# A routed mixture of experts on one core: one table value per tile, expert weights in two unpadded parts, rows as 16-bit halves

## What is computed

```python
h = _layernorm(x, axis=-1) * (1 + cb) + sb
x = x + gb * _L0_ffn_ref(h, ...)

# _L0_ffn_ref: 32 experts in 4 groups, M = 176 hidden values
scores = sigmoid(x @ gate_w)                     # best 2 of 4 groups, in them the best 6 experts
weights = picked scores / their sum
g = ragged_dot(xs, w_gate, group_sizes)          # xs: each token once for each of its 6 experts,
u = ragged_dot(xs, w_up, group_sizes)            #     sorted by expert
d = ragged_dot(silu(g) * u, w_down, group_sizes)
expert_out = sum over the token's 6 rows of d * weights
shared = silu(x @ sw_gate) * (x @ sw_up) @ sw_down
```

## Time and profile before

| | us |
|---|---|
| median of 3 runs | 1948.27 (1947.77 to 1954.84) |
| the profiled execution, its own time | 1951.45 |
| its span, first to last instruction | 1949.6 |

### The profile page before, as it was taken

One profiled execution on the slowest core, in us unless ns is written; L12 is line 12 of the kernel. 1 busy time (PEld: TensorE's weight loads), 2 busy tenths in 40 slices (PEclk: granted clock), 3 DMA queues, 4 the chain that ended last, 5 costly groups with the idle time before them and its releaser, 6 DMA issues. The chain is left out here.

```text
span 1949.6 us, 43870 instructions
## 1 busy us (share of the span) xinstructions
PE 1851.4 (95%) x13730; PEld 981.7 (50%) x13730; DVE 1254.6 (64%) x2826; ACT 1384.7 (71%) x1908; POOL 1383.7 (71%) x837
## 2 busy tenths in 40 slices
PE   8979999999999999999999999999889689999986
PEld 6734444444444444444444444444376467777765
DVE  5777777767776777677767776776076345555553
ACT  5617888888888888888888888888752145555543
POOL 1526888988898889888988898889747723333330
PEclk9969999999999999999999999999999889999998
DMA  6100122112111211121112211000024379999979
GB/s 251 49 10 1 65 98 89 66 63 112 74 66 63 110 76 66 63 110 76 66 63 108 78 66 52 8 6 10 7 86 184 135 247 345 338 350 354 346 270 302
DMA packets 104645, 240.00 MB, mean 123 GB/s; under 512 B 24656, under 2 KB 57680, under 8 KB 104464
## 3 DMA queue, kind: packets, MB, share of 16 engines
q1 hardware_dynamic: 93840, 209.18, 30.2%
q0 software_dynamic: 10752, 30.16, 4.0%
HBM read 130.66 MB, written 104.37 MB: 121 GB/s over the span
## 5 line engine op out<-in xcount | busy, mean ns | idle before, releaser
L899 POOL TENSOR_TENSOR prob_lo<-prob,prob_hi 128x1024 f16<-128x1024 f32 x512 | 1080.8, 2129 | 166.4 <-ACT prob_hi L928 166.4
L974 DVE TENSOR_REDUCE maxes<-ring 128x1 f32<-128x512 f32 x1024 | 645.2, 684 | 232.4 <-PE ring L1065 229.9
L926 ACT ACTIVATE prob<-p_s,prob_scale 128x1024 f32<-128x1024 f32 x512 | 571.1, 1115 | 212.2 <-PE p_s L1084 190.7
L928 ACT ACTIVATE prob_hi<-p_s,prob_scale 128x1024 f16<-128x1024 f32 x512 | 570.3, 1114 | 0.0
L1065 PE MATMUL ring<-kr_hi,qr_hi 64*128 64x512 f16 x1024 | 374.8, 384 | 7.7 <-DVE qc_hi L961 4.2
L1065 PE MATMUL ring<-kc_pair,qc_hi 64*128 64x512 f16 x1024 | 371.3, 383 | 0.0
L1084 PE MATMUL p_s<-qr_lo,kr_hi 64*128 64x512 f16 x1024 | 287.0, 375 | 0.0
L1084 PE MATMUL p_s<-qr_hi,kr_lo 64*128 64x512 f16 x1024 | 286.5, 376 | 0.0
L1353 POOL DMA_INDIRECT ranked_out<-y,dest x128 | 123.1, 962 | 216.2 <-DVE y L1660 213.5
L1084 PE MATMUL p_s<-qr_hi,kr_hi 64*128 64x512 f16 x1024 | 244.2, 380 | 1.6 <-ACT prob_hi L928 1.6
L1084 PE MATMUL p_s<-qc_lo,kc_one 33*128 33x512 f16 x1024 | 242.4, 378 | 0.0
(11 more groups left out here) (248 smaller groups left out, 2447.4 us busy)
## 6 DMA issues: line engine op xcount, KB each, us to landing
w<-in_experts SPq DMA_DIRECT2D x128, 608.0 KB, 5.3
expert_rows<-zeros SPq DMA_DIRECT2D x129, 544.0 KB, 4.7
rows<-expert_rows SPq DMA_DIRECT2D x128, 136.0 KB, 4.7
got<-ranked_out SPq DMA_DIRECT2D x16, 768.0 KB, 10.4
wqb<-in_wqb SPq DMA_DIRECT2D x8, 768.0 KB, 4.9
recip_wide<-prob_recips SPq DMA_DIRECT2D x64, 64.0 KB
cbar<-att_t SPq DMA_DIRECT2D x64, 64.0 KB, 2.0
cbar<-in_woT SPq DMA_DIRECT2D x1, 2048.0 KB, 16.8
```

The costliest lines, as they stand in the source:

```text
L899: gp.tensor_tensor(prob_lo[s % NB][:, :], prob[s % 2][:, :], prob_hi[s % NB][:, :], ALU.subtract).then_inc(lo_ready, 1)
L926: act.activation(prob[s % 2][:, :], p_s[s % 2][:, :], ACT.Exp, bias=prob_scale[:, :], scale=SCALE / W_SCALE)
L928: act.activation(prob_hi[s % NB][:, :], p_s[s % 2][:, :], ACT.Exp, bias=prob_scale[:, :], scale=SCALE / W_SCALE).then_inc(p_ready, 1)
L974: best = v.tensor_reduce(maxes[:, at:at + 1], bank[:, :], AX.X, ALU.max)
```

## The change

There are three parts.

1. SyncE reads one table value per tile, the first row, and gets the expert as that row divided by S. The second table, its spread on VectorE and half of the spread product on TensorE are gone.
2. The weights lie in DRAM as two arrays: `experts_long`, 96 rows of 704 + 512 values, and `experts_short`, 32 rows of 704. Each tile's (and each shared half's) weights are two DMAs, into rows 0 to 95 of the buffer and into the first 704 columns of rows 96 to 127. The waits count to twice as much.
3. The normalized rows are kept in float32 in the (still unused) weight buffers. ScalarE copies them as 16-bit floats into the first half of the row's 256 words (`pairs`), ahead of the modulation; VectorE subtracts that half from the float32 row and stores the rest as 16-bit floats in the second half (`low_half`), for tile t - 5 in rounds 5 to 11 and for the last nine tiles between the shared expert's units. `turn_h` reads the float32 rows. In `turn_rows` four 16-bit products against a 16-bit identity take the place of the two transposes; those of the high and the low half add up in one bank.

```diff
 def _(sp):
             for n in range(2):
-                sp.dma_start(ws[n][:, :], a["experts"][E + n, :, :]).then_inc(ld_ws, 16)
+                sp.dma_start(ws[n][0:WROWS, :], a["experts_long"][E + n, :, :]).then_inc(ld_ws, 16)
+                sp.dma_start(ws[n][WROWS:P, 0:WIN], a["experts_short"][E + n, :, :]).then_inc(ld_ws, 16)
...
+            def first_row(i, u):
+                return sp.value_load(tile_row[0:1, ds(i + u, 1)], min_val=0, max_val=E * S)
+
+            def load_weights(i, u, r):
+                e = ds(r // S, 1)
                 sp.wait_ge(y_mm, i + u + 1)
-                sp.dma_start(w[u][:, :], a["experts"][ds(e, 1), :, :].rearrange("a p n -> (a p) n")).then_inc(w_ld[u], 16)
-
-            def load_rows(i, u, first=False):
-                r = sp.value_load(tile_row[0:1, ds(i + u, 1)], min_val=0, max_val=E * S)
+                sp.dma_start(w[u][0:WROWS, :], a["experts_long"][e, :, :].rearrange("a p n -> (a p) n")).then_inc(w_ld[u], 16)
+                sp.dma_start(w[u][WROWS:P, 0:WIN], a["experts_short"][e, :, :].rearrange("a p n -> (a p) n")).then_inc(w_ld[u], 16)
+
+            def load_rows(i, u, r, first=False):
...
             with sp.Fori(1, SLOT_TILES // U) as trip_no:
                 i = trip_no * U
                 for u in range(U):
-                    load_weights(i, u)
-                    load_rows(i, u)
+                    r = first_row(i, u)
+                    load_weights(i, u, r)
+                    load_rows(i, u, r)
 def _(act):
                 if 2 <= t <= T + 1:
                     act.wait_ge(t_mm, t - 1)
+                    act.copy(pairs[t - 2][:, 0:D], normed[t - 2])
                     modulate(h2T[:, (t - 2) * D:(t - 1) * D], p_t[t % 2], t_ready)
 def _(v):
-                v.tensor_scalar(hall[:, t * RW:t * RW + D], xt, mv[:, t * 2:t * 2 + 1], rstd[:, t:t + 1],
+                v.tensor_scalar(normed[t], xt, mv[:, t * 2:t * 2 + 1], rstd[:, t:t + 1],
                                 ALU.subtract, ALU.mult).then_inc(h_ready, 1)
+
+            def low_half(t):
+
+                v.wait_ge(t_ready, t + 1)
+                v.tensor_tensor(pairs[t][:, D:2 * D], normed[t], pairs[t][:, 0:D], ALU.subtract)
...
+                if 5 <= t < 5 + GROUP[END][0]:
+                    low_half(t - 5)
...
+                for t in range(GROUP[END][0] + 2 * n, min(GROUP[END][0] + 2 * n + 2, T)):
+                    low_half(t)
 def _(pe):
             def turn_rows(n, u, ring):
                 pe.wait_ge(row_ld[u % U], ring)
                 pe.wait_ge(r_used, n + 1)
+                pair = rows[u % U][:, 0:D].bitcast(F16)
                 for k in range(DK):
-                    last = pe.transpose(p_r[u % 2][:, k * P:(k + 1) * P], rows[u % U][:, k * P:(k + 1) * P], ident[:, :])
+                    for half in range(2):
+                        at = half * D + k * P
+                        last = pe.matmul(p_r[u % 2][:, k * P:(k + 1) * P], pair[:, at:at + P], ident16[:, :],
+                                         start=(half == 0), stop=(half == 1))
                 last.then_inc(r_mm, 1)
...
-                pe.wait_ge(w_ld[u % U], ring)
+                pe.wait_ge(w_ld[u % U], 2 * ring)
```

More of the change, by code:

```diff
@@ L44 @@
 WIN = DK * 2 * M
+WROWS = 96
 WOUT = 2 * D
@@ L1203, in mixture @@
         tcol = sb("tcol", 4)
-        spread = sb("spread", 2 * P)
+        spread = sb("spread", P)
         own_slot = sb("own_slot", SLOT_TILES)
         tile_row = sb("tile_row", SLOT_TILES, I32, parts=1)
-        tile_expert = sb("tile_expert", SLOT_TILES, I32, parts=1)
         wsum = sb("wsum", T)
@@ L1273, in mixture @@
         ranked = [sem(f"ranked{n}") for n in range(U)]
+        ident16 = sb("ident16", P, F16)
+        normed = [w[t // 4][:, t % 4 * D:(t % 4 + 1) * D] for t in range(T)]
+        pairs = [hall[:, t * RW:t * RW + D].bitcast(F16) for t in range(T)]
         block = st.enter_context(nc.Block())
@@ L1292, in _ @@
             for n in range(2):
-                sp.dma_start(ws[n][:, :], a["experts"][E + n, :, :]).then_inc(ld_ws, 16)
+                sp.dma_start(ws[n][0:WROWS, :], a["experts_long"][E + n, :, :]).then_inc(ld_ws, 16)
+                sp.dma_start(ws[n][WROWS:P, 0:WIN], a["experts_short"][E + n, :, :]).then_inc(ld_ws, 16)
             sp.wait_ge(answered, 2 * last + 2)
             store_heads(sp, last, scaling, cbar, stored)
-            def load_weights(i, u):
-                e = sp.value_load(tile_expert[0:1, ds(i + u, 1)], min_val=0, max_val=E - 1)
+            def first_row(i, u):
+                return sp.value_load(tile_row[0:1, ds(i + u, 1)], min_val=0, max_val=E * S)
+            def load_weights(i, u, r):
+                e = ds(r // S, 1)
                 sp.wait_ge(y_mm, i + u + 1)
-                sp.dma_start(w[u][:, :], a["experts"][ds(e, 1), :, :].rearrange("a p n -> (a p) n")).then_inc(w_ld[u], 16)
-            def load_rows(i, u, first=False):
-                r = sp.value_load(tile_row[0:1, ds(i + u, 1)], min_val=0, max_val=E * S)
+                sp.dma_start(w[u][0:WROWS, :], a["experts_long"][e, :, :].rearrange("a p n -> (a p) n")).then_inc(w_ld[u], 16)
+                sp.dma_start(w[u][WROWS:P, 0:WIN], a["experts_short"][e, :, :].rearrange("a p n -> (a p) n")).then_inc(w_ld[u], 16)
+            def load_rows(i, u, r, first=False):
                 if not first:
@@ L1306, in load_rows @@
                 sp.dma_start(rows[u][:, :], slots_dram[ds(r, P), :]).then_inc(row_ld[u], 16)
-            sp.wait_ge(tables, 2)
+            sp.wait_ge(tables, 1)
             for u in range(U):
-                load_weights(0, u)
+                load_weights(0, u, first_row(0, u))
             sp.wait_ge(scattered, 16 * TOPK * T)
             for u in range(U):
-                load_rows(0, u, first=True)
+                load_rows(0, u, first_row(0, u), first=True)
             with sp.Fori(1, SLOT_TILES // U) as trip_no:
@@ L1333, in _ @@
             gp.wait_ge(pads, 2)
-            gp.wait_ge(ld_ws, 32)
+            gp.wait_ge(ld_ws, 64)
             for n in range(2):
@@ L1564, in tile_table @@
                 step(v.tensor_scalar(tcol[:, 2:3], tcol[:, 2:3], float(E * S), None, ALU.min))
-                step(v.tensor_scalar(tcol[:, 3:4], tcol[:, 0:1], float(E - 1), None, ALU.min))
-                step(v.tensor_scalar(spread[:, 0:P], ident[:, :], tcol[:, 2:3], None, ALU.mult))
-                v.tensor_scalar(spread[:, P:2 * P], ident[:, :], tcol[:, 3:4], None, ALU.mult).then_inc(spread_ready, 1)
+                v.tensor_scalar(spread[:, :], ident[:, :], tcol[:, 2:3], None, ALU.mult).then_inc(spread_ready, 1)
             def keep_table():
@@ L1572, in keep_table @@
                 v.tensor_copy(tile_row[0:1, :], p_l[0:1, 0:P]).then_inc(tables, 1)
-                v.tensor_copy(tile_expert[0:1, :], p_l[0:1, P:2 * P]).then_inc(tables, 1)
             def weigh_tokens(j):
@@ L1586, in weigh_tokens @@
                 step(v.tensor_reduce(t3(weight, 8)[:, :, j], t3(pick), AX.X, ALU.add))
+            step(v.tensor_copy(ident16[:, :], ident[:, :]))
             v.wait_ge(col_mm, 1)
@@ L1698, in turn_h @@
                 for k in range(DK):
-                    last = pe.transpose(p_t[t % 2][:, k * P:(k + 1) * P], hall[:, t * RW + k * P:t * RW + (k + 1) * P],
-                                        ident[:, :])
+                    last = pe.transpose(p_t[t % 2][:, k * P:(k + 1) * P], normed[t][:, k * P:(k + 1) * P], ident[:, :])
                 last.then_inc(t_mm, 1)
@@ L1739, in spread_table @@
                 pe.wait_ge(spread_ready, 1)
-                pe.matmul(p_l[:, 0:2 * P], ones[:, :], spread[:, :], start=True, stop=True).then_inc(spread_mm, 1)
+                pe.matmul(p_l[:, 0:P], ones[:, :], spread[:, :], start=True, stop=True).then_inc(spread_mm, 1)
             for n, part in enumerate((4, 4, 3, 3)):
@@ L1783, in shared_down @@
                 last.then_inc(sd_mm, 1)
-            pe.wait_ge(ld_ws, 32)
+            pe.wait_ge(ld_ws, 64)
             pe.wait_ge(folded, 2)
@@ L1841, in trip @@
                 down(n, u)
-            pe.wait_ge(tables, 2)
+            pe.wait_ge(tables, 1)
             pe.wait_ge(s_added, T)
@@ L1966 @@
     w_down = np.concatenate([given["L0_ffn_w_down"], sw_down.reshape(2, M, D)])
-    w_out = np.zeros((E + 2, P, WOUT), f32)
+    w_out = np.zeros((E + 2, WROWS, WOUT), f32)
     w_out[:, :MH] = w_down.reshape(E + 2, 2, MH, D).transpose(0, 2, 1, 3).reshape(E + 2, MH, WOUT)
@@ L1983 @@
         "gate": given["L0_ffn_gate_w"],
-        "experts": np.concatenate([w_in, w_out], axis=2),
+        "experts_long": np.concatenate([w_in[:, :WROWS], w_out], axis=2),
+        "experts_short": w_in[:, WROWS:],
         "lower": np.triu(np.ones((P, P), f32), 1),
```

## The result

| | before | after |
|---|---|---|
| median of the runs, us | 1949.26 (1947.77 to 1954.84) | 1991.32 (1985.07 to 2000.3) |
| the profiled execution, its own time | 1951.45 | 1987.79 |
| its span | 1949.6 | 1985.7 |
| ratio of the times, 95% interval | | 1.0207 (1.0181 to 1.0232) |

The kernel before has one run more here than in the first table. The change makes the kernel 2.1% slower. I had forecast no measurable difference, and the time lies outside my range.

A forecast was written before the change was run, and what follows sets the result against it. SyncE's issuing was taken to bound the routed loop once TensorE's lead was gone, GpSimd's scatters its start. Loop -6.7 and routing +2.0 gave -4.7 us, a predicted median of 1943.6 us, range 1939.5 to 1960.5.

The forecast's parts named there:

- DMA engines: Routed loop: 827 kB a tile at 346 GB/s takes 2.39 us, below TensorE and SyncE; at 323 GB/s 2.56.
- Rival C: Loop gains nothing: saved load exchanged for a DMA, or parts at 323 GB/s (+1.1 us); 1950 to 1951; chance 0.11.
- TensorE: Routed loop: turning rows stays at 0.22 us at most, a tile at 2.49 us; from tile 8 -7.4 us.
- Rival A: Weight loads show in the turn's four 16-bit products, 0.10 us each: 2.68 us a tile, 1966.9 us; chance 0.16.
- SyncE: Loop issuing: one table load less, one weight DMA and quotient operation more; 2.51 us a tile, ends 2.44 and 2.75.
- B: SyncE gets slower in the loop: three quotient operations, 2.66 us a tile, 1959.7 us; longer DMA too, 1970; chance 0.10.
- the lead: Before the change: rows issued ahead of TensorE's need; shrinks 0.09 us a tile, gone after some 37 tiles.
- Routing: VectorE's subtractions and ScalarE's copies delay the second group's slots and scatters: +2.0 us, ends 0.5 and 3.9.
- At no cost: Last group's nine subtractions and three copies, 5.2 us, covered by 8.4 us while GpSimd scatters the second group.
- The sum: Whole kernel: loop -6.7 and routing +2.0 give -4.7 us, predicted median 1943.6 us.

The follow-up runs named there:

- columns_96: Changed kernel with weights as two loads: gate and up columns of 128 rows, down columns of 96 rows (544 KB); ratio 0.9999 to the kernel before.
- columns: Changed kernel with weights as two loads of all 128 rows, gate and up columns and padded down columns; ratio 0.999 to the kernel before.
- whole_load: Changed kernel with each tile's weights again as one padded load of 128 rows (608 KB); ratio 0.9989 to the kernel before.
- one_value: Kernel before with the single table value per tile alone, whole padded weights, 32-bit rows; ratio 0.9933 to the kernel before.
- one_value_again: The kernel of one_value run again on another chip; ratio 0.9961 to the kernel before, 2.490 us a tile.
- one_value_columns: Kernel with one table value per tile and 32-bit rows, weights cut as in columns_96; ratio 1.0008 to the kernel before.
- turn_first: whole_load with TensorE turning the rows ahead of the hidden values; ratio 0.9973 to the kernel before, 2.495 us a tile.

## Why the prediction was wrong

*DMA engines: the step that failed.* I put 827 kB at 346 GB/s, 2.39 us a tile, with 323 GB/s as the lower bound, from the nearest row of a lower rate. Measured: 295 GB/s, 2.82 us. I took the rate as a property of the engines and the bytes, when it belongs to the layout of each load: in the rows I had, every load covers all 128 partitions, so none of them could bound one that doesn't. Even without slower packets the step was wrong in kind. The 64 rows that partitions 0 to 63 take were as many and as long as before; the 64 KB saved came off the other half. `columns_96` shows what such a saving is worth: the same 64 KB less than in `columns`, and the same share of 1.02. Rival C had named the place (the parts at a lower rate) and priced it at +1.1 us instead of the loop's +31.35. What would have shown it was what came: share over 1.00, landings of 8 to 10 us.

*TensorE: the turn was right, the tile was not.* The turn takes 1590.27 - 1590.05 = 0.22 us, as forecast. But I looked at what covers the 16-bit loads and not at what the 16-bit products have to cover. The next 32-bit load sticks out: 2.548 - 2.490 = 0.058 us a tile, 119 times, 6.9 us; hidden in the changed kernel by the DMA, plain in whole_load. Rival A's 0.10 us a product didn't come: four took 0.22 us. The Trainium skill's 81 ns for a pair of load and product (TensorE: Matmul & The Clock Gate, Back-to-back issue gap) didn't come either.

*SyncE.* Forecast 2.51 us a tile; (240 - 33.5) / 85 = 2.43. The second DMA lasts 0.32 us and one operation makes the quotient, so B fell. (By my own 0.065 us an operation, two more of them would have cost 0.13 and not the 0.15 in B.) That SyncE's pace was the bound before is confirmed: with less to do in one_value, all 119 tiles take 2.49. In the trace of before the 2.49 holds up to tile 40, near the 37 tiles from tile 8 that I had given the lead.

*Routing.* Forecast +2.0 (0.5 to 3.9). The second group's first scatter:

```profile
1455.91 0.96 POOL L1352 DMA_INDIRECT expert_rows<-hall,slot  x1 [8.24 <-DVE slot L1556]
```

1455.91 - 1452.47 = 3.44 us later, and the first turn 2.81 later. Not all of the 3.44 is the change's. Counted from VectorE's first addition to `x`, that scatter comes after 43.0 us before and 46.4 after, but after 43.6 in one_value_again and 44.8 in one_value_columns, neither of which has the halves. So 1.6 to 3.4 us are theirs: the mechanism fits, and +2.0 was right or a little low.

*At no cost.* GpSimd waits for slots only twice in its 96 scatters (the view of line L1352: 14.2 us, 2 times), so the last group's subtractions stayed covered, but only just. Its slots come 10.1 us later than before, at 1492.9, and the group's first scatter at 1494.46; in turn_first, with the same halves, GpSimd does wait for them (17.8 us, 3 times). The +1.79 us of the first eight tiles I had not forecast, and they can't be put down to the change: that stretch takes 18.9 to 22.7 us in the runs. one_value_again, which has no pairs of loads, has 1586.60 - 1564.60 = 22.00 us there instead of 20.50 (1585.45 - 1564.95).

*The sum.* Without the parts, what is left is whole_load: ratio 0.9989, interval up to 1.0002. My -4.7 with the 6.9 of the uncovered load would be +2.2, or 1.001, a little too high; the single value is worth more than I gave it, 0.4 to 0.7% alone, and why that differs between the two chips I can't say.

Open stays how the 16 engines share the rows of a load among them, and with that the exact size of the slowing; the trace doesn't tell the engines apart.

## What to carry to other kernels

A DMA's cost is not its bytes: ask which partitions it covers, and don't cut a load of 128 rows at row 96 or 64, not even to save zeros. When a product is made cheaper, look at the weight load behind it, which may have been hidden under it. And where a change has three parts, price and try them one by one: here the single table value was worth 0.4 to 0.7%, the 16-bit halves cost 0.6 and the two parts of the weights over 2.

## What was new about the hardware

- Loads onto partitions 0 to 63 slow the packets of all others too (rows' from 48 to 88 ns in the median). Loads onto 32 to 95 or the even ones leave those at 48, though they too raise the results' from 159 to 175 and 178.
- Unequal cover can be free at one pace and not at the next: the 96-row load of the down columns did no harm to the time at 2.548 us a tile; with TensorE at 2.49 the tiles from the 80th on took 2.69.
- The packets' share can stand at 1.05 while the rate, 295 GB/s, is 15% below the 346 at 0.98: the share is no measure of bytes.
- An issue of 64 rows of 4,864 bytes takes SyncE 0.47 to 0.55 us, one of 96 or 128 rows 0.32 to 0.33.
- Four 16-bit products of 128 columns with their weight loads take 0.22 us; a 32-bit load of 0.19 us behind one of them costs 0.055.
